# A planner's start time for VectorE: 24 in place of 44, in a four-layer graph network on one core

## The reference, cut to what matters

```
x = ln(x + attention0(x[src], edge_attr, x[dst]))          # softmax over the edges of one dst, sums into dst
x = ln(x + ln2(mlp(ln1(gelu(attention1(x[src], x[dst])) + x))))   # 64 -> 128 -> 64 for all 100000 nodes
x = ln(x + (sum over dst==row of x[src] / sqrt(deg deg)) @ W.T + b)   # degree over src, sums into src
x = ln(x + sum over src==row of edge_weight * x[dst] ...)
```

## Time and profile before

| what | value |
|---|---|
| time, median of 3 runs | 2683.65 us (2670.19 to 2685.36) |
| profiled execution | 2680.65 us, its span 2678.8 us |
| busy in the span | PE 67%, DVE 64%, ACT 55%, POOL 63% |
| granted TensorE clock, mean | 0.829 |
| chain that ended last | POOL 16% of the span, issue 6%, ACT 4%, DVE 4%, PE 4% |

### The profile page before, as it was taken

One profiled execution on the slowest core, in us unless ns is written; L12 is line 12 of the kernel. 1 busy time (PEld: TensorE's weight loads), 2 busy tenths in 40 slices (PEclk: granted clock), 3 DMA queues, 4 the chain that ended last, 5 costly groups with the idle time before them and its releaser, 6 DMA issues. The chain is left out here.

```text
span 2678.8 us, 24741 instructions
## 1 busy us (share of the span) xinstructions
PE 1807.6 (67%) x7450; PEld 868.5 (32%) x7450; DVE 1724.8 (64%) x3305; ACT 1465.7 (55%) x2212; POOL 1679.7 (63%) x1610
## 2 busy tenths in 40 slices
PE   5999989767977888898999876568877654000000
PEld 3444444324533333344444324433322343000000
DVE  5888989988888787765555469887666775000002
ACT  3787777753676667677777755357777521000000
POOL 5777777710057771006777578775777787777774
PEclk9999999987997888899999986679999755555555
DMA  3333222214622221124444644432121233000002
GB/s 68 73 75 80 68 72 64 63 31 126 192 77 49 60 55 32 47 77 113 138 129 135 179 150 124 117 78 65 58 58 54 86 106 110 16 18 21 22 21 99
DMA packets 236808, 214.81 MB, mean 80 GB/s; under 512 B 157822, under 2 KB 170965, under 8 KB 236677
## 3 DMA queue, kind: packets, MB, share of 16 engines
q1 hardware_dynamic: 182228, 166.60, 21.7%
q0 software_dynamic: 51200, 46.31, 7.2%
q10 hardware_dynamic: 3248, 0.34, 0.1%
HBM read 140.36 MB, written 86.31 MB: 85 GB/s over the span
## 5 line engine op out<-in xcount | busy, mean ns | idle before, releaser
L2405 POOL DMA_INDIRECT stab<-wk,rank_i x200 | 215.0, 1075 | 267.4 <-DVE wk L621 209.1
L578 ACT ACTIVATE b_s<-ps,vec 128x512 f32<-128x512 f32 (+1 forms) x356 | 240.8, 682 | 137.7 <-PE ps L572 45.0
L2402 POOL DMA_INDIRECT e_bc<-x0tab,dpos_i x136 | 137.7, 1013 | 245.7 <-DMA x0tab<-e_bc 200.6
L2402 POOL DMA_INDIRECT u<-x2tab,dpos_i x200 | 227.8, 1139 | 80.2 <-issue 75.3
L809 DVE TENSOR_SCALAR b_x<-b_s 128x8 f32<-128x8 f32 x2 | 0.3, 167 | 396.4 <-DMA b_gl<-out_dram 396.4
L2402 POOL DMA_INDIRECT u<-x3tab,src_i x200 | 206.1, 1030 | 78.8 <-issue 59.4
L2402 POOL DMA_INDIRECT u<-in_x_dram,src_i x200 | 201.7, 1009 | 76.7 <-issue 56.9
L2402 POOL DMA_INDIRECT u<-in_x_dram,dst_i x200 | 207.7, 1038 | 64.3 <-issue 60.9
L2405 POOL DMA_INDIRECT out_dram<-u,sfin_i x200 | 196.5, 982 | 66.3 <-issue 66.3
L2405 POOL DMA_INDIRECT out_dram<-u,dst_i x176 | 197.2, 1120 | 60.6 <-issue 56.0
L566 PE MATMUL ps<-b_h,blk_c 128*128 128x512 f32 (+1 forms) x296 | 169.3, 655 | 35.6 <-ACT b_gl L586 35.1
(11 more groups left out here) (423 smaller groups left out, 4747.4 us busy)
## 6 DMA issues: line engine op xcount, KB each, us to landing
b_gl<-in_x_dram SPq DMA_DIRECT2D x98, 256.0 KB, 2.8
wk<-dlist SPq DMA_DIRECT2D x50, 500.0 KB
wk<-slist SPq DMA_DIRECT2D x50, 500.0 KB
out_dram<-b_gl SPq DMA_DIRECT2D x93, 256.0 KB, 2.0
u<-stab SPq DMA_DIRECT2D x25, 510.0 KB
x2none<-b_gl SPq DMA_DIRECT2D x25, 250.0 KB
x0tab<-e_bc SPq DMA_DIRECT2D x25, 240.0 KB
wk<-x2none SPq DMA_DIRECT2D x25, 240.0 KB
```

The source lines that it names most:

```text
L578: return nc.scalar.activation(b_s[l][:, 0:w], pB[l][:, 0:w], ACT.Abs_reciprocal_sqrt, bias=col(EPSV))
L2402: pool.indirect_dma_start(out=o, out_offset=None, in_=tab, in_offset=at_ix(ix), **kw).then_inc(s, 16)
L2405: pool.indirect_dma_start(out=tab, out_offset=at_ix(ix), in_=a, in_offset=None, bounds_check=last, oob_is_err=False).then_inc(s, 16)
```

## The change

One number is changed: the time from which the planner takes VectorE to be free. Those of TensorE and ScalarE stay, and with them those of the lanes and banks.

```diff
-        START = dict(pe=44.0, act=44.0, dve=44.0, pool=16.0, sp=0.0)
+        START = dict(pe=44.0, act=44.0, dve=24.0, pool=16.0, sp=0.0)
```

## The result

The changed kernel took 2654.29 us (median of 6 runs, 2647.64 to 2659.51) against 2680.13 us for the kernel before in the same comparison (2670.19 to 2688.83): ratio 0.9901 [0.9883, 0.9920]. The sign was right, but most of the gain came from places that the sum had put at nothing; that they gained was luck, as far as the forecast goes.

A forecast was written before the change was run, and what follows sets the result against it. The prediction took POOL's gather and scatter chain, stretched by two pauses, as the bound; -5.6 us in the first pause plus 0.5 for POOL gave -5.1, so 2678 us from the median 2683.65, range 2657 to 2699.

The forecast's parts named there:

- the sum: Whole run: -5.6 us in the first pause plus 0.5 for POOL, -5.1; late start and later phases at nothing.
- The late start: Start of the kernel: index steps ahead delay setup by 9.3 us, hidden by later waits and costed at nothing.
- the cover of the earlier trace: DVE's waits for u2's gathers, 5.54 and 4.97 us, 10.5 together, taken to hide setup's 9.3 us delay.
- the slower rival: DVE's order between 370 and 554 us: setup's delay comes through, at most 9.3 us, 2693 with the gain lost; chance 0.13.
- the 558 that the forecast had named as a sign of being wrong: End of u2: the forecast is wrong if the softmax begins later than 558 us.
- The gain in the first pause: Before u3: index sort ends earlier, so layer 0's first five group intervals shorten; gain 5.6 us, between 0 and 10.8.
- POOL beside a busier DVE: u1's gathers, 27.4 to 44.8 us: about 14 gathers slowed by 0.033 us each, costing 0.5 us, at most 4.1.
- The rival of the port: u1's gathers: full blocking costs 4.1 us, leaving -1.5 and 2682 us; chance 0.05.
- the rule: SBUF access: a two-input VectorE instruction and a GpSimd instruction reading SBUF contend, the later one fully blocked.
- The plan gets luckier: Layer 0's groups around prep2: it may fall where groups wait anyway, saving 6.1 us more, 2672 us; chance 0.13.
- the rival of the second pause: Pause before u4: replanned orders change its 193.6 us by 27, to 2657 or 2711; chance 0.05 faster, 0.04 slower.
- the 10 that the forecast had named as a sign of being wrong: Pause before u4: the forecast is wrong if it differs from 193.6 us by more than 10 us.

The follow-up runs named there:

- experiment 1: Kernel before with its old plan; only the first 27 index steps get the new, earlier times, ahead of setup. 2678.4 us, ratio 0.9997.
- experiment 2: Changed kernel with its new plan, but setup's two parts issued ahead of the index sort and its stages. 2653.78 us, ratio 0.9912.
- 3: Kernel before with a long hold: no dense block enters a lane from layer 0's sum of group 22 to the last source tile. 2618.58 us.
- 5: Kernel before with a short hold: dense blocks kept out from layer 0's sum of group 22 only until the sixth source tile. 2671.04 us.
- Experiment 4: Changed kernel with 12 us of delay in the planner's dependencies of the first five source tiles. 2677.47 us, ratio 0.9991.
- 42: Kernel before with VectorE's start time in the planner at 42 in place of 44. 2656.9 us, ratio 0.9908.
- 36: Kernel before with VectorE's start time in the planner at 36 in place of 44. 2655.24 us, ratio 0.9891.
- 34: Kernel before with VectorE's start time in the planner at 34 in place of 44. 2812.31 us, ratio 1.0480.
- 26: Kernel before with VectorE's start time in the planner at 26 in place of 44. 2676.36 us, ratio 0.9997.

## Why the prediction was wrong

**The late start: right.** It was 8.1 us, not 9.3 (`prep_dve` ended 1.3 us earlier in this execution). DVE's waits for u2's gathers between 300 and 560 us, the cover of the earlier trace rows, were 14.5 us in five waits before, and are these now:

```profile
DVE q_b L1137 <- DMA u<-in_x_dram,dst_i: 0.7, 1, 0.7
```

The cover was nearly used up, as the slower rival feared, but only in part by the late start. With the late start and the old plan (experiment 1) 6.3 us of it are left, 8.2 less for a start 8.6 us later, which is the forecast's argument at work; with the new plan and an early setup (experiment 2) 2.5 are left. Softmax 0 began 3 us later (560.91 for 557.87), past the 558 that the forecast had named as a sign of being wrong; but u2's last gather itself began 2.2 us later, and in experiment 2, where setup is early, later still (556.3). Experiments 1 and 2 show no cost of the late start.

**The gain in the first pause: right in place, and in size where it was counted.** The five intervals lost 6.0 us for the forecast 5.6; in the four traces with the old plan up to there they take 28.3 to 29.1 us, in the four with the new one 22.2. The sort's end moved 44 us, not 18 to 27, both before the first output. Windows over these intervals, before and after (columns as above):

```profile
630.73:659.01 28.28, 17.66 (x127) 14.65 (x128) 25.14 (x47) 4.71 (x8) 0.00 (x0) 0.70 0.50 152
```

```profile
632.50:654.75 22.25, 22.25 (x150) 12.65 (x148) 19.76 (x29) 16.43 (x22) 0.00 (x0) 1.00 0.64 196
```

DVE was busy 25.1 us before, 10.7 of it with the sort, and 19.8 after: the sort's steps are gone, and other steps, dense ones among them, took half of their place. But TensorE's clock was granted at 0.70 of full there before and at 1.00 after, and no run changed the one without the other, so that the sort alone gave the 6.0 us is argued and not shown. The 4.6 us in the later groups were not forecast. Part of them may be the clock too, granted at 1.00 over these groups and at 0.94 before; the split is open. u3 starts between 750.4 and 757.0 in experiments 1, 3 and 5, whose plan is the old one up to there, and at 748.3 and 746.5 in 2 and 4 with the new one, so u3's 8.8 is known to some 3 us.

**POOL beside a busier DVE: too high.** 14 gathers between 27 and 43.5 us took 958 ns each after and 954 before; 4 ns each, 0.06 us in place of 0.5, with DVE busy for 15.3 of these 16.5 us in place of 8.4, and no sign of a full block. The rival of the port falls: what the forecast took from the rule does not hold for these gathers.

**The plan gets luckier: fell.** The 10.7-us interval is still there, from 670.30 to 680.95 in the rows above, 60 us earlier than in the earlier trace rows. prep2 changed its place and kept its cost.

**The step that failed:** "The index loads, the second pause and all later phases start earlier by as much and are costed at nothing, since their order is planned from the same dependencies". The dependencies are the same and the order is not. The planner takes, greedily, whatever step can start first, and a dense block that takes a lane a moment earlier or later holds it for tens of us. After u3's start the changed kernel gained 12.3 us in the source stage, 0.6 between it and u4, 5.8 in u4's stage and 5.8 behind it. Experiment 1 has the old order there once more, experiment 2 the new one, and they tell what of this is clear of the noise: the source stage is (333.8 and 340.8 us with the old order, 321.5 and 319.7 with the new), u4's is not (287.7 and 284.9 against 281.9 and 284.2), and behind u4 the two are 3 to 13 us apart, which no experiment looked into. Experiment 4 takes the source stage's gain away while the sort stays early; 42 and 36 bring a gain behind u3 with less head start; 34 turns it into a loss.

This was the rival of the second pause, put at 27 us either way and given 0.05 and 0.04. Its mechanism was right and its chance far too small. Its size was right for the neighbours rather than for 24: the stretch from u3's start to u4's moved by 12.9 us with 24, 18.8 with 42, 20.4 with 36 and 32.0 with 26, and u4's stage by 150 with 34. The pause itself became 12.2 us shorter with 24, past the 10 that the forecast had named as a sign of being wrong.

The trace before had the evidence. The forecast took POOL to issue "without long pauses" within a phase, which is true of its gathers (u3 is done at 1020.7), but u4 waits for the tiles, and those end at 1085.8, 65 us after u3's last gather begins (54 in the changed kernel, 20 with the hold). That lag, and scores 25 us apart where gathers allow 10.4, could have been read from it. DVE's score copies waited 24.2 us for ScalarE before, 23.0 after and 2.3 with the hold.

The new plan itself, which is made before any run, could have been read too: the expectations for 42, 26, 34 and 36 were read off the lanes' times in it, and three of the four measured times lie in the range so found and the fourth 2 us outside (26 by another way than expected).

**What stays open:** what each dense block costs. By L719 the source stage has three of them before and after, and the number alone does not give the length (three: 333.8 and 321.5 us; two, in the short hold: 320.0; four: 344.8 in experiment 4, the last near its end, and 325.6 with 42; none: 281.1 and 272.6). Their places matter too: one block ahead of the first tile goes with the 12.3 us, and experiment 4 puts one back there, but it moves other blocks as well, and no run moved a single block alone.

## What to carry to other kernels

When a change alters an input of a greedy planner, everything behind it is drawn anew: price that draw by the scatter of neighbouring values (here 2654 to 2812 us), and ask for a run with the new plan and the old cause before believing the cause. In the trace, compare a stage's length with its gathers' own: here the tiles lagged far behind, filler work in shared lanes was the bound, and holding it back (2619 us alone, 2613 with the new start time) was worth more than the change under study. And read the new plan before forecasting from the old trace.

## What was not expected of the hardware

TensorE's clock has two levels, 1.2 and 2.4 GHz. In the source stage it was granted at 0.84 of full on average before, 0.83 after and 0.93 with the hold, although the hold gives TensorE no more work there (busy 216 of 281 us, for 263 of 334 before). The tiles' matmuls of 128 x 500 followed it. As groups (busy us, mean ns, idle before), before and with the hold:

```profile
L833 PE MATMUL ps<-b_s,blk_j 128*128 128x500 f32 x50 | 43.0, 957 | 0.0
```

```profile
L833 PE MATMUL ps<-b_s,blk_j 128*128 128x500 f32 x50 | 28.0, 644 | 0.0
```

The same matmul took 957 and 644 ns on average, by a profile that models a matmul's end. The averages hide two values: about 625 ns in stretches granted at 2.4 GHz and about 1100 at 1.2. Before, 12 of the 50 ran wholly at the higher level and 31 at the lower; with the hold, 48 and 2. The tiles' own matmuls thus ran faster without dense blocks among them; how much of the 52.7 us is that, and how much the lanes, was not separated.
